# The edge loop of a graph network on one core: target rows gathered with an add onto source rows, four slots of one pair

## The reference, cut to what matters

```python
row, col = (edge_index[0], edge_index[1])
m = jnp.concatenate([x[row], x[col]], axis=1)
m = jax.nn.relu(m @ Wm1 + bm1)                     # 256 -> 256, per edge
m = jax.nn.relu(m @ Wm2 + bm2)                     # 256 -> 256, per edge
m_sum = jax.ops.segment_sum(m, row, num_segments=x.shape[0])
```

## Time and profile before

| What | Value |
|---|---|
| three timed runs | 1084.2, 1084.83 and 1084.91 us, median 1084.83 |
| the profiled execution | 1082.0 us, of which its span is 1080.2 |
| mean granted clock of TensorE | 0.875 of full speed |
| PE busy | 847.7 us (78% of the span) |
| DVE busy | 699.8 us (65%) |
| ACT busy | 549.2 us (51%) |
| POOL busy | 496.9 us (46%) |
| transfers | 44.23 MB, of them 37.77 MB gathered in the edge loop |

### The profile page before, as it was taken

One profiled execution on the slowest core, in us unless ns is written; L12 is line 12 of the kernel. 1 busy time (PEld: TensorE's weight loads), 2 busy tenths in 40 slices (PEclk: granted clock), 3 DMA queues, 4 the chain that ended last, 5 costly groups with the idle time before them and its releaser, 6 DMA issues.

```text
span 1080.2 us, 19301 instructions
## 1 busy us (share of the span) xinstructions
PE 847.7 (78%) x4594; PEld 544.0 (50%) x4595; DVE 699.8 (65%) x1997; ACT 549.2 (51%) x1043; POOL 496.9 (46%) x406
## 2 busy tenths in 40 slices
PE   3999977877887888888878788796686677768777
PEld 2777455655665666666656566372223221412144
DVE  8899734454544545454454545769976997799681
ACT  2311234344444444444444444648884888389832
POOL 0000354545445555555544455036970797089600
PEclk9999988899889889888897888889878978886898
DMA  2400122222122122222221224000000000000000
GB/s 69 139 1 1 39 69 68 73 63 78 53 63 78 58 78 63 73 63 73 73 63 58 62 72 69 12 1 1 0 1 0 1 1 0 1 1 1 1 1 20
DMA packets 24112, 44.23 MB, mean 41 GB/s; under 512 B 7185, under 2 KB 14354, under 8 KB 24082
## 3 DMA queue, kind: packets, MB, share of 16 engines
q0 software_dynamic: 13824, 37.77, 12.2%
q1 hardware_dynamic: 10258, 6.11, 2.0%
HBM read 41.23 MB, written 2.62 MB: 41 GB/s over the span
## 4 chain that ended last, share of the span: by engine, by line
PE 50%; DVE 20%; issue 15%; ACT 5%; another core or an unknown queue 5%; POOL 2%; ACTq 1%; DMA 1%; DVEq 0%; POOLq 0%
PE PS L1155 6%; PE PS L1231 6%; PE PS L1232 6%; PE PS L1299 5%; PE PS L1310 5%; DVE scratch L993 4%; DVE hots L993 4%; PE PS L1220 3%; PE PS L1296 2%; PE PS L1443 2%; PE PS L1228 2%; PE PS L1238 2%; PE PS L1521 2%; ACT Ur L454 1%
## 5 line engine op out<-in xcount | busy, mean ns | idle before, releaser
L322 POOL DMA_INDIRECT G<-Ptab,stg x144 | 139.9, 971 | 305.0 <-DVE edge L871 155.9
L322 POOL DMA_INDIRECT G<-Qtab,stg x144 | 146.8, 1020 | 43.9 <-issue 42.0
L465 ACT ACTIVATE late<-PS 128x512 f32 (+1 forms) x69 | 41.2, 596 | 241.1 <-remote 119.0
L454 ACT ACTIVATE Ur<-hots,sew x408 | 127.0, 390 | 27.2 <-issue 27.2
L1443 PE MATMUL PS<-G,HX 128*33 128x512 f32 x264 | 86.0, 755 | 46.4 <-POOL G L384 38.2
L384 POOL TENSOR_TENSOR G<-cntf,CT 128x1024 f32<-128x1024 f32 x30 | 72.1, 2403 | 95.2 <-ACT cntf L593 92.2
L1299 PE MATMUL PS<-OHd,Ur 128*128 x852 | 104.4, 242 | 10.2 <-issue 9.4
L1231 PE MATMUL PS<-Wm,edge 128*128 128x256 f32 x276 | 99.2, 447 | 0.0
L922 DVE TENSOR_SCALAR hots<-early,srcl 128x128 f16 x136 | 32.3, 279 | 100.4 <-remote 44.6
L1232 PE MATMUL PS<-Wm,edge 128*128 128x256 f32 x276 | 96.4, 436 | 0.0
L871 DVE TENSOR_TENSOR edge<-G 128x512 f32 x68 | 47.0, 691 | 76.3 <-PE PS L1220 41.8
(11 more groups left out here) (336 smaller groups left out, 1875.4 us busy)
## 6 DMA issues: line engine op xcount, KB each, us to landing
G<-Ptab,stg POOLq DMA_INDIRECT x144
G<-Qtab,stg POOLq DMA_INDIRECT x144
Ptab<-BT SPq DMA_DIRECT2D x1, 1024.0 KB, 4.7
Qtab<-BT SPq DMA_DIRECT2D x1, 1024.0 KB, 7.6
SKT<-in_L_gnn_Wn SPq DMA_DIRECT2D x1, 1024.0 KB, 5.3
x<-in_x SPq DMA_DIRECT2D x1, 512.0 KB, 3.9
Wm<-in_L_gnn_Wm SPq DMA_DIRECT2D x2, 256.0 KB
early<-in_L_gnn_W SPq DMA_DIRECT2D x4, 64.0 KB, 3.2
```

Of the source, the lines that this page charges most:

```text
L322: g.indirect_dma_start(out=G[:, s, t, k, :], out_offset=None, in_=(Ptab, Qtab)[t], in_offset=bass.IndirectOffsetOnAxis(ap=stg[:, s, 2 * t ...
L454: last = a.activation(part_of(slot, k, j), onehot(slot, k), ACT.Copy, scale=sew[:, j, bass.ds(2 * g + k, 1)])
```

## The change

`G` keeps its 16 KB per partition, but is now four slots of one pair each, where a slot holds only two chunks: the sum of source and target rows. POOL gathers the two source chunks into a slot as before. The two target chunks are gathered into the same place with `compute_op=ALU.add`, so that the DMA adds each fetched row to what lies there. Before it may do so, POOL waits until the source rows have landed. In a step of the loop POOL issues the sources of pair p, waits for the finished sums of pair p-2, waits for the sources of pair p-1, and issues its two target gathers. DVE's message is no longer an add of two halves but a copy of the slot, scaled by 1.0. The number of gathers stays at four per pair, and so does the number of pairs that are asked for, 72. `stg` has four slots as well, so four sets of row numbers are written ahead of the loop, and `rounds` counts groups of four pairs.

The rest is names: three semaphores are taken together with others (`act_step` with `pairs_asked`, `norms` with `squares`, `none_part` with `none_ready`). None of their waits changes its meaning.

```diff
-NASK = NPAIR + 4
+NASK = NPAIR + 6
+SLOTS = 4
...
-        stg = sb("stg", [P, 2, 4], u32)
-        G = sb("G", [P, 2, 2, 2, F2])
+        stg = sb("stg", [P, SLOTS, 4], u32)
+        G = sb("G", [P, SLOTS, 2, F2])
...
-            def rows(s, t, k):
-
-                g.indirect_dma_start(
-                    out=G[:, s, t, k, :], out_offset=None, in_=(Ptab, Qtab)[t],
-                    in_offset=bass.IndirectOffsetOnAxis(ap=stg[:, s, 2 * t + k:2 * t + k + 1], axis=0),
-                ).then_inc(S(f"slot{s}_landed"), 16)
-
-            def gather(i, s):
-
-                eng.wait_ge(S("stg_ready"), 2 * i + s + 1)
-                eng.wait_ge(S("msg_ready"), 2 * i - 1 + s)
+            def sources(s):
+
+                for k in range(2):
+                    g.indirect_dma_start(
+                        out=G[:, s, k, :], out_offset=None, in_=Ptab,
+                        in_offset=bass.IndirectOffsetOnAxis(ap=stg[:, s, k:k + 1], axis=0),
+                    ).then_inc(S(f"slot{s}_landed"), 16)
+
+            def targets_added(s):
+
+                for k in range(2):
+                    g.indirect_dma_start(
+                        out=G[:, s, k, :], out_offset=None, in_=Qtab,
+                        in_offset=bass.IndirectOffsetOnAxis(ap=stg[:, s, 2 + k:3 + k], axis=0), compute_op=ALU.add,
+                    ).then_inc(S(f"slot{s}_landed"), 16)
+
+            def sums_landed(s, turns, more):
+
+                eng.wait_ge(S(f"slot{s % SLOTS}_landed"), 64 * turns + 64 * more)
+                g.sem_inc(S("gathered"), 1)
+
+            def sources_landed(s, turns, more):
+
+                eng.wait_ge(S(f"slot{s % SLOTS}_landed"), 64 * turns + (64 * more - 32))
                 g.sem_inc(S("pairs_asked"), 1)
-                rows(s, 0, 0)
-                rows(s, 0, 1)
-                rows(s, 1, 0)
-                eng.wait_ge(S(f"slot{1 - s}_landed"), 64 * i + 64 * s)
-                g.sem_inc(S("gathered"), 1)
-                rows(s, 1, 1)
...
+            sources(0)
+            sources(1)
+            sources_landed(0, 0, 1)
+            targets_added(0)
+            sources(2)
+            sums_landed(0, 0, 1)
+            sources_landed(1, 0, 1)
+            targets_added(1)
+            sources(3)
+            sums_landed(1, 0, 1)
+            sources_landed(2, 0, 1)
+            targets_added(2)
+            with eng.Fori(0, rounds) as i:
+                for s in range(SLOTS):
+                    eng.wait_ge(S("stg_ready"), SLOTS * i + (SLOTS + s + 1))
+                    eng.wait_ge(S("msg_ready"), SLOTS * i + (s + 1))
+                    g.sem_inc(S("pairs_asked"), 1)
+                    sources(s)
+                    sums_landed(s - 2, i, 2 if s >= 2 else 1)
+                    sources_landed(s - 1, i, 2 if s >= 1 else 1)
+                    targets_added((s - 1) % SLOTS)
...
             def second_layer(slot):
 
-                a.sem_inc(S("act_step"), 1)
+                a.sem_inc(S("pairs_asked"), 1)
...
             def message(g):
 
-                slot = g & 1
+                slot = g & (SLOTS - 1)
                 eng.wait_ge(S("gathered"), g + 2)
-                indices(g + 2, slot)
+                indices(g + SLOTS, slot)
                 eng.wait_ge(S("t_done"), g)
-                v.tensor_tensor(MS[:].rearrange("p k f -> p (k f)"),
-                                G[:, bass.ds(slot, 1), 0, :, :].rearrange("p o k f -> p (o k f)"),
-                                G[:, bass.ds(slot, 1), 1, :, :].rearrange("p o k f -> p (o k f)"),
-                                ALU.add).then_inc(S("msg_ready"), 1)
+                v.tensor_scalar(MS[:].rearrange("p k f -> p (k f)"),
+                                G[:, bass.ds(slot, 1), :, :].rearrange("p o k f -> p (o k f)"), 1.0, None,
+                                ALU.mult).then_inc(S("msg_ready"), 1)
```

More of the change, by code:

```diff
@@ L229, in gnn_kernel @@
         Eb = [cntf[:], hnT[:], Wm[:].rearrange("p w k f -> p (w k f)")]
-        EC = [G[:, i, :, :, :].rearrange("p t k f -> p (t k f)") for i in range(2)]\
+        EC = [gflat[:, i * N:(i + 1) * N] for i in range(2)]\
             + [edge[:].rearrange("p i f -> p (i f)")]
@@ L327, in gather @@
-            def gather(i, s):
-                eng.wait_ge(S("stg_ready"), 2 * i + s + 1)
-                eng.wait_ge(S("msg_ready"), 2 * i - 1 + s)
-                g.sem_inc(S("pairs_asked"), 1)
-                rows(s, 0, 0)
-                rows(s, 0, 1)
-                rows(s, 1, 0)
-                eng.wait_ge(S(f"slot{1 - s}_landed"), 64 * i + 64 * s)
-                g.sem_inc(S("gathered"), 1)
-                rows(s, 1, 1)
-            eng.wait_ge(S("stg_ready"), 2)
-            for t in range(2):
-                for k in range(2):
-                    rows(0, t, k)
@@ L343, in _ @@
-            g.sem_inc(S("gathered"), 1)
-            for t in range(2):
-                for k in range(2):
-                    rows(1, t, k)
-            eng.wait_ge(S("slot0_landed"), 64)
-            g.sem_inc(S("gathered"), 1)
-            with eng.Fori(1, rounds) as i:
-                gather(i, 0)
-                gather(i, 1)
-            eng.wait_ge(S("slot1_landed"), 64 * rounds)
-            g.sem_inc(S("gathered"), 1)
-            eng.wait_ge(S("slot0_landed"), 64 * rounds)
+            def sources(s):
[4 more added lines that the diff above has]
+                    ).then_inc(S(f"slot{s}_landed"), 16)
@@ L355, in _ @@
+            sums_landed(SLOTS - 2, rounds, 1)
+            sources_landed(SLOTS - 1, rounds, 1)
+            targets_added(SLOTS - 1)
+            sums_landed(SLOTS - 1, rounds, 1)
             g.sem_inc(S("gathers_over"), 1)
@@ L399, in _ @@
                 eng.wait_ge(S("squares"), b + 1)
-            a.activation(nrm[:], ssq[:], ACT.Sqrt).then_inc(S("norms"), 1)
+            a.activation(nrm[:], ssq[:], ACT.Sqrt).then_inc(S("squares"), 1)
             eng.wait_ge(S("ln0_Tp"), 1)
@@ L759, in _ @@
             link(v.tensor_copy(tabs[:, NB:2 * NB], pb[:]))
-            link(v.tensor_scalar(off[:, 0:1], pb[:, NB - 1:NB], 4.0, None, ALU.add))
+            link(v.tensor_scalar(off[:, 0:1], pb[:, NB - 1:NB], 2.0, None, ALU.add))
             link(v.tensor_copy(npi[:, 0:1], off[:, 0:1]))
-            link(v.tensor_scalar(tabs[:, 2 * NB:2 * NB + 1], npi[:, 0:1], 1, None, ALU.arith_shift_right))
+            link(v.tensor_scalar(tabs[:, 2 * NB:2 * NB + 1], npi[:, 0:1], 2, None, ALU.arith_shift_right))
             link(v.tensor_tensor(pb[:], pb[:], npf[:], ALU.subtract))
@@ L803, in _ @@
             eng.wait_ge(S("indices_ready"), 2)
-            for slot in range(2):
+            for slot in range(SLOTS):
                 indices(slot, slot)
@@ L860, in _ @@
             eng.wait_ge(S("gathered"), 2)
[L861 to L862 removed]
+            indices(SLOTS, 0)
+            v.tensor_scalar(MS[:], G[:, 0, :, :], 1.0, None, ALU.mult).then_inc(S("msg_ready"), 1)
             def message(g):
[L867 removed]
+                slot = g & (SLOTS - 1)
                 eng.wait_ge(S("gathered"), g + 2)
[L869 removed]
+                indices(g + SLOTS, slot)
                 eng.wait_ge(S("t_done"), g)
[L871 to L874 removed]
+                v.tensor_scalar(MS[:].rearrange("p k f -> p (k f)"),
+                                G[:, bass.ds(slot, 1), :, :].rearrange("p o k f -> p (o k f)"), 1.0, None,
+                                ALU.mult).then_inc(S("msg_ready"), 1)
             local = lambda pair, k: srcl[:, bass.ds(2 * pair + k, 1)]
@@ L896, in _ @@
             eng.wait_ge(S("gathered"), 3)
-            indices(3, 1)
+            indices(SLOTS + 1, 1)
             eng.wait_ge(S("t_done"), 1)
-            v.tensor_tensor(MS[:], G[:, 1, 0, :, :], G[:, 1, 1, :, :], ALU.add).then_inc(S("msg_ready"), 1)
+            v.tensor_scalar(MS[:], G[:, 1, :, :], 1.0, None, ALU.mult).then_inc(S("msg_ready"), 1)
             eng.wait_ge(S("ranks_done"), 1)
@@ L906, in _ @@
             eng.wait_ge(S("gathered"), 4)
-            indices(4, 0)
+            indices(SLOTS + 2, 2)
             eng.wait_ge(S("t_done"), 2)
-            v.tensor_tensor(MS[:], G[:, 0, 0, :, :], G[:, 0, 1, :, :], ALU.add).then_inc(S("msg_ready"), 1)
+            v.tensor_scalar(MS[:], G[:, 2, :, :], 1.0, None, ALU.mult).then_inc(S("msg_ready"), 1)
             with eng.Fori(0, NB) as b:
```

19 lines of the change are left out of this document (9 added, 10 removed).

## The result

The changed kernel takes 1014.7 us (median of 4 runs, 1013.4 to 1017.3), the kernel before beside it 1084.9: ratio 0.935, 95% interval 0.932 to 0.938. Two later pairs of runs gave 0.9375 (0.9335 to 0.9414) and 0.934 (0.928 to 0.940). It is 70 us faster, where 1110 us was forecast. No step of the prediction uses it.)

A forecast was written before the change was run, and what follows sets the result against it. PE's path with holds, not POOL, was taken to bound the loop. Holds +25.6, prologue +1.0 and end -1.8 gave +24.8 on 1082.0; with 2.8 for the median, 1110 us, own range 1097 to 1122, 8 in 10 1062 to 1165.

The forecast's parts named there:

- The bound before: Edge loop, 494.5 of 1080.2 us: PE busy 82% and 50% of the last chain; POOL has room.
- holds: Edge loop: engine waits ending when the group's last gather lands; 26, each 0.985 us longer, +25.6 us (-6.9 to +54.7).
- The add gather: POOL's target gathers with add: 1.43 us each in place of 0.953, making a group 5.95 us in place of 5.0.
- The four slots: Edge loop: messages free a slot four pairs ahead; the reserve hides nothing that was exposed, taken as 0.
- Rival 3: Edge loop: four slots shorten the holds by moving groups away from PE's signals; 1050 us, chance 0.12.
- All the rivals: Four alternatives for the whole kernel: 1076 us (chance 0.20), 1157 (0.15), 1050 (0.12) and 1084 (0.13).
- The message: DVE's one-input copy: 426 ns in place of 691, counted only at holds, 26 x 0.265 = -6.9 us.
- The port: DVE's copy making POOL's gathers wait in the loop: at most 11 us more, taken as 0.
- The lock-out of the Trainium skill: Rule that DVE in 2-port mode and POOL lock each other out for an instruction; would add 11 us, not counted.
- Prologue: Before the loop: more indices and a second sum ready after ten gathers, 3 to 4 us later; counted +1.0 (0 to +4).
- End: After the last gather: ACT's 1.82 us wait goes because the last pair is asked for two messages earlier, -1.8 us.

The follow-up runs named there:

- g2: Kernel before with only the two source gathers per pair and a message copying them (target part left out): 953.9 us, ratio 0.882.
- f4: Kernel before, three semaphore names merged, with a POOL memset of 128x128 behind each gather: 1068.8 us, ratio 0.989.
- f1: Kernel before, three semaphore names merged, with a POOL memset of 128x256 behind each gather: 1047.2 us, ratio 0.971.
- f2: Kernel before, three semaphore names merged, with four POOL memsets of 128x256 behind each group's fourth gather: 1037.9 us, ratio 0.961.
- f5: Kernel before, three semaphore names merged, with five POOL memsets of 128x256 behind each group of gathers: 1029.5 us, ratio 0.951.
- e1: Changed kernel with plain target gathers, no add (source part of the sum left out): 1092.8 us, ratio 1.008 to the kernel before.
- g3: Changed kernel with plain target gathers (source part left out) and five memsets of 128x256 behind each step: 1030.5 us, ratio 0.952.
- e2: Changed kernel, but POOL waits for one message more before each group, so at most three slots are in use: 1021.4 us, ratio 0.943.
- e4: Kernel before with the message as a copy of the source half alone (target part left out): 1089.6 us, ratio 1.003.
- j2: The kernel of g4 run again on a chip where the kernel before took 1086.8 us: 1032.0 us, ratio 0.950.
- g4: Changed kernel, plain target gathers (source part left out), 640 columns of memsets behind each; chip where before took 955.5: 986.7 us, ratio 1.033.

## Why the prediction was wrong

**The bound before.** That PE's path sets the loop and that holds cost it time was right; g2 gives their price, 1083 to 954, and the kernel before itself took 955.5 where no holds showed. That includes a slower clock behind stalls. Here are the hold of the earlier trace rows and what followed, as windows of before:

```profile
388.00:391.00 3.00, 1.16 (x10) 0.84 (x9) 0.69 (x1) 1.60 (x5) 0.37 (x2) 1.00 0.19 66
392.00:395.00 3.00, 3.00 (x10) 2.41 (x9) 2.36 (x11) 1.70 (x4) 2.23 (x3) 0.50 0.30 87
```

PE was busy for 1.16 of 3 us, and then ran at the lower of its two clock levels, 0.50. PE's busy time for the same matmuls is 421.9 us in the loop of before and 372.8 in g2.

**The step that failed** is the one on holds: "26 holds, each later by 0.95 (group) + 0.3 (landing) - 0.265 (message)", +25.6 us, and before it the sentence that the hold is a coupling through which a longer gather group reaches PE's path. It took the number of holds as given and let the group lengthen each. The runs show the reverse: the changed kernel has 14.5 us in 4 pieces in place of 115.1 in 26 ahead of ACT's second-layer eviction, and a longer step of POOL, by nothing but memsets, makes the loop shorter (f4, f1, f2, f5 in order) and takes "remote" waits away (f2, f5). Where +24.8 us was forecast, the change gave -70. The hold's end at the last landing was read rightly, and its cause wrongly. It is not one wait that ends with a landing: in e1's trace PE gets through between the bursts, late in a dense run of gathers.

**The add gather**, 1.43 us by my estimate, is 1.57, and the group 6.35 in place of 5.95. The direction was right. With plain gathers the gain is gone (e1), so this slower gather, which the prediction priced as a loss, is what the gain needs.

**The four slots**, taken as 0, are 0 at equal pace: g3 and f5 differ by 1 us, e1 is 1% slower than before. With the adds, holding one of the four back costs 7 us (e2), about what POOL then waits for messages (6.5 us). Rival 3, whose 1050 us was nearest, put the gain on the slots: right in sign, wrong in cause. All the rivals kept "POOL's time costs or is hidden"; none had it that a slower POOL helps.

**The message**, 0.426 us by the rows, is 0.427; its -6.9 us did not show (e4). **The port**, 0: the source gathers' median went from 0.95 to 1.01, and e4, which has the one-input copy and nothing else of the change, does not tell itself from before. e1 has that copy too and its source gathers stay at 0.955, so the 0.05 us goes with the adds and not with the copy. The lock-out of the Trainium skill ("SBUF — State Buffer", "Who interferes with whom") is for these gathers neither shown nor excluded at this size.

**Prologue.** Forecast +1.0. The second message came at 139.8 in place of 134.5, 5.3 us later where 3 to 4 were forecast: the prediction has the second sum ready after ten gathers, but in the listing of the change POOL counts it only behind twelve. Even so, the loop's first message was earlier, at 153.4 in place of 156.6: -3.2. **End.** Forecast -1.8. ACT's wait for `gathers_over` is 10.1 us in place of 1.8, since POOL is now behind, and L529 starts 6.8 us after the last message in place of 4.9: +1.8. Both are small.

**Settled:** the gain needs the slower pace; slots, names and message are not it; bytes do not matter, the number of gathers (with their rows) does. **Open:** why an add gather does 15 us better than plain gathers with memsets at the same step (g3, j2), by what path gathers hold up the other engines, and why one session, on one chip, shows no holds: chip, moment and placement of the tables were not told apart. The changed kernel was not run on that chip. g4, with nearly the same step, lost 3.3% there, so I expect it to lose as well, which no run shows. No kernel that forms the whole sum was found to be faster than the changed one; g2 says where to look, in fewer gathers for each pair.

## What to carry to other kernels

When all engines pause together and resume in the gaps of indirect gathers, try making the gathers sparser before making them cheaper: a few memsets on the issuing engine are a test of one line, and here they were worth 5%. Halve the count of gathers in another test, since count and not bytes was the price here. And time such a result on more than one chip, because a gain that lies in removed pauses may be gone where there are none.

## What the runs showed of the hardware

- A gather of 128 rows takes POOL 0.95 us with rows of 1 KB or of 512 B, 0.91 (sources) and 1.06 us (targets) with 64 rows, and 1.57 us with the add. With the add in half of the gathers the queue's packets double, from 13824 to 27648.
- Late in a run of eight gathers 1.26 us apart (e1, from 436.7 us), PE, ACT and DVE stood for most of the time in which bytes moved; PE issued single transposes 1.4 us apart there. At 6.25 us for four gathers the loop was 42 us (f5) shorter than at 5.07.
- Behind a hold in the kernel before (PE busy 1.16 of 3 us) the granted clock of TensorE was 0.50 in 392 to 395 us, and two matmuls of L1232 took 1.06 us in place of 0.59.
- The same program, the kernel before, took 1081 to 1087 us beside all other runs and 955.5 in one session on one chip: 12% less, more than the change itself gives.
